# A state-space scan, a 4-bit FFN and a mixture layer in one kernel: contiguous scale and zero-point rows, and output product and expert-input turns moved into the second scan

## What is computed

```
x  = x + ln(mamba(ln(x)))       # conv, selective scan over 512 steps, 1024 x 16 states, gate, y @ W_out.T
x  = x + ln16(gptq_ffn(ln(x)))  # w = q*s[g] - (z[g]+1)*s[g]; down(silu(gate(x)) * up(x)), inner width 1376
x  = x + ln(attention(ln(x)))   # per token, 32 heads of 16
x  = x + ln(moe(ln(x)))
```

## Time and profile before

| | |
|---|---|
| median of 3 runs | 893.2 us (892.1 to 893.83) |
| profiled execution | 893.42 us, its span 891.5 us |
| mean granted TensorE clock | 0.881 |
| TensorE busy | 701.6 us (79%) |
| VectorE busy | 715.8 us (80%) |
| GpSimd busy | 542.7 us (61%) |
| ScalarE busy | 420.6 us (47%) |
| DMA | 86.72 MB, 97 GB/s over the span; 18308 of 65212 packets under 512 B |

### The profile page before, as it was taken

One profiled execution on the slowest core, in us unless ns is written; L12 is line 12 of the kernel. 1 busy time (PEld: TensorE's weight loads), 2 busy tenths in 40 slices (PEclk: granted clock), 3 DMA queues, 4 the chain that ended last, 5 costly groups with the idle time before them and its releaser, 6 DMA issues. The chain is left out here.

```text
span 891.5 us, 8190 instructions
## 1 busy us (share of the span) xinstructions
PE 701.6 (79%) x2700; PEld 316.2 (35%) x2700; DVE 715.8 (80%) x719; ACT 420.6 (47%) x699; POOL 542.7 (61%) x281
## 2 busy tenths in 40 slices
PE   6986669998766978346643499798999978999895
PEld 3322123332211322011110144343445534787774
DVE  4846999989999999999999896988464573676657
ACT  2344776687646764555544224333334343522331
POOL 0008899989989999899999555577002031341152
PEclk9998868999878999567775599899999989999998
DMA  9102423331425432673322067983300020000011
GB/s 277 45 26 102 149 76 100 119 118 56 180 97 183 148 117 84 183 207 118 118 89 77 18 144 193 251 200 79 142 0 1 1 96 0 1 1 1 1 47 48
DMA packets 65212, 86.72 MB, mean 97 GB/s; under 512 B 18308, under 2 KB 32407, under 8 KB 64914
## 3 DMA queue, kind: packets, MB, share of 16 engines
q1 hardware_dynamic: 65170, 86.20, 32.0%
HBM read 74.97 MB, written 11.21 MB: 97 GB/s over the span
## 5 line engine op out<-in xcount | busy, mean ns | idle before, releaser
L1965 POOL TENSOR_TENSOR dbu<-rep_du,bc 128x1024 f32<-128x1024 f32 x128 | 299.0, 2358 | 6.4 <-DVE psum L1066 3.7
L1645 ACT ACTIVATE psum<-rep_dt,aneg 128x512 f32<-128x512 f32 x256 | 166.1, 682 | 148.2 <-DVE hc L1077 118.9
L1066 DVE TENSOR_TENSOR_SCAN psum<-psum,dbu 128x1024 f32<-128x1024 f32 x87 | 198.7, 2284 | 7.7 <-ACT psum L1645 5.1
L845 PE MATMUL psum<-hc,stk 128*32 128x512 f32 x512 | 91.8, 798 | 75.9 <-POOL hc L1974 38.0
L1077 DVE TENSOR_TENSOR hc<-psum,bc 128x1024 f32<-128x1024 f32 x87 | 106.5, 1224 | 3.4 <-PE psum L845 0.4
L1974 POOL TENSOR_TENSOR hc<-hc,bc 128x1024 f32<-128x1024 f32 x41 | 96.5, 2354 | 11.6 <-DVE hc L1066 11.4
L1066 DVE TENSOR_TENSOR_SCAN hc<-psum,dbu 128x1024 f32<-128x1024 f32 x41 | 93.5, 2280 | 6.6 <-ACT psum L1645 4.2
L642 PE MATMUL psum<-xf_hi,gu_hi 128*128 128x512 f16 x176 | 67.7, 385 | 0.0
L642 PE MATMUL psum<-xf_hi,gu_lo 128*128 128x512 f16 x176 | 67.4, 383 | 0.0
L642 PE MATMUL psum<-xf_lo,gu_hi 128*128 128x512 f16 x176 | 67.2, 382 | 0.0
L642 PE MATMUL psum<-xT,w_g 128*128 128x512 f32 x120 | 59.4, 640 | 6.9 <-DVE dt_t L1085 6.9
(11 more groups left out here) (225 smaller groups left out, 1399.1 us busy)
## 6 DMA issues: line engine op xcount, KB each, us to landing
rep_dt<-rep_scratch SPq DMA_DIRECT2D x60, 256.0 KB, 3.3
rep_du<-rep_scratch SPq DMA_DIRECT2D x60, 256.0 KB, 4.3
q_gu<-qgu_in SPq DMA_DIRECT2D x11, 512.0 KB, 4.5
z_gu<-zgu_scratch SPq DMA_DIRECT2D x11, 512.0 KB, 6.6
bc<-bc_scratch SPq DMA_DIRECT2D x16, 256.0 KB, 4.3
rep_scratch<-du_t SPq DMA_DIRECT2D x15, 256.0 KB, 2.0
rep_scratch<-dt_t SPq DMA_DIRECT2D x15, 256.0 KB, 2.3
q_d<-qd_in SPq DMA_DIRECT2D x11, 256.0 KB, 5.0
```

Of the source, the lines that this page charges most:

```text
L845: last = pe.matmul(y_rows(k), stk[:], hc[:, (i + k // 2) % HCS, k % 2, :], start=False, stop=(s == GN - 1))
L1066: dve.tensor_tensor_scan(h, a, dbu[:, i % DBS].rearrange("p e t -> p (e t)"), 0.0, ALU.mult, ALU.add)\
L1645: last = act.activation(psum[:, 2 * (i % 2) + e, :], rep_dt[:, cc % 2, k, :], ACT.Exp, scale=aneg[:, k, c, n:n + 1])
L1965: pool.tensor_tensor(dbu[:, i % DBS], rep_du[:, cc % 2, k:k + 2, :], bc[:, n, :].unsqueeze(1).broadcast_to([P, 2, L]), ALU.mult).then_inc( ...
```

## The change

- Scales and zero points are written once, early, into two scratch arrays with one contiguous row of 1536 values per chunk; a stage has four transfers. There are four slots (`SLOTS`); the fourth lies where batch 1's y was.
- The input of the FFN of batch 0 is normed by ScalarE, turned by TensorE and split by ScalarE and VectorE in scan chunks 13 and 14.
- The output product of batch 1 over inner chunks 0 to 5 (`part`, `PARTS` = 6 of 8) moves into chunks 14 and 15. ScalarE copies it to `obuf`; the other two inner chunks remain at the seam, and VectorE adds the two (`add_partial`).
- The merging of the expert matrices moves one chunk earlier, and its buffers to another place.
- The first `unpack` stands between the last pair and the last `take_y`. Ahead of the first round three chunks are unpacked, not four, and in the rounds VectorE runs `low_weights(i + 2)` and then `unpack(i + 3)`.
- GpSimd does `d_lo` of chunk i-1 after `w_gu` and `w_d` of chunk i. ScalarE waits for `w_gu` and `w_d` separately.
- SyncE loads the attention's weights after the last stage; their two reductions on VectorE stand in round 9, not 7.

The core of the diff:

```diff
+SZ = 2 * KH * P + H
+SLOTS = 4
...
-        (11, 1): [("ft", 0)], (11, 2): [("ft", 1)], (11, 3): [("w1", 0)], (12, 1): [("w1", 1)],
-        (12, 3): [("wr", 0)], (13, 1): [("wr", 1)], (13, 2): [("wr", 2)], (13, 3): [("wr", 3)]}
+        (10, 1): [("ft", 0)], (10, 2): [("ft", 1)], (11, 1): [("w1", 0)], (11, 2): [("w1", 1)],
+        (11, 3): [("wr", 0)], (12, 1): [("wr", 1)], (12, 2): [("wr", 2)], (12, 3): [("wr", 3)],
+        (13, 0): [("tr", "ffn", 0, 0)], (13, 1): [("tr", "ffn", 0, 1)], (13, 3): [("tr", "ffn", 0, 2)],
+        (14, 0): [("tr", "ffn", 0, 3)],
+        (14, 1): [("part", 0)], (14, 2): [("part", 1)], (14, 3): [("part", 2)], (15, 1): [("part", 3)]}
+PARTS = DC - 2
...
+                load(scl[s][:], s_dram[i:i + 1, :].broadcast_to([P, SZ]), ld_stage[s])
+                load(zp[s][:], z_dram[i:i + 1, :].broadcast_to([P, SZ]), ld_stage[s])
...
             for h in range(KH):
                 wait_taken(sp_, ("wr", h))
                 sp_.dma_start(wr_dram[h * P:(h + 1) * P, :], wr_t[h][:]).then_inc(wr_stored, 16)
+            sp_.wait_ge(wr_stored, 16 * KH)
+            stage(1)
...
+            def out_partial(t):
+
+                item = ("part", t)
+                pe.wait_ge(y_taken, DC + PARTS)
+                start(item)
+                product(item, [(u0[:, c, t * P:(t + 1) * P], wout[:, c, :]) for c in range(PARTS)])\
+                    .then_inc(work_ready, 1)
...
+                for t in range(NT):
+                    if i == pair_of(("tr", "ffn", 0, t)) + 3:
+                        low_turned(0, [t])
+            unpack(0)
             take_y(NCH - 1)
...
+            def add_partial(t):
+                item = ("out", 1, t)
+                wait_work(dve, item)
+                wait_taken(dve, ("part", t))
+                dve.tensor_tensor(obuf[1][:, t, :], bank(item), obuf[1][:, t, :], ALU.add)\
+                    .then_inc(taken_sem(item), 1)
+
+            unpack(1)
+            low_weights(0)
             for t in range(NT):
-                norm_tile("ffn", 0, t, xnc)
-            low_turned(0)
-            unpack(0)
-            for i in range(1, 4):
-                unpack(i)
-                low_weights(i - 1)
+                add_partial(t)
+            unpack(2)
+            low_weights(1)
             for i in range(IC):
                 ffn_inner(0, i)
...
-                if i + 4 < IC:
-                    unpack(i + 4)
+                if i + 2 < IC:
+                    low_weights(i + 2)
                 if i + 3 < IC:
-                    low_weights(i + 3)
+                    unpack(i + 3)
...
-                act.wait_ge(w_done, 2 * (i + 1))
-                act.copy(gu_hi[:, i, :], w_gu[i % 3][:]).then_inc(whi_done, 1)
-                act.copy(d_hi[:, i, :], w_d[i % 3][:]).then_inc(whi_done, 1)
+                act.wait_ge(w_done, 2 * i + 1)
+                act.copy(gu_hi[:, i, :], w_gu[i % SLOTS][:]).then_inc(whi_done, 1)
+                act.wait_ge(w_done, 2 * i + 2)
+                act.copy(d_hi[:, i, :], w_d[i % SLOTS][:]).then_inc(whi_done, 1)
...
+            act.wait_ge(exp_done, NPAIR)
+            for i in range(3):
+                high_weights(i)
...
+                pool.wait_ge(q_done, 2 * i + 1)
+                pool.tensor_tensor(w_gu[s][:], w_gu[s][:], z_gu[s], ALU.subtract).then_inc(w_done, 1)
                 pool.wait_ge(q_done, 2 * i + 2)
+                pool.tensor_tensor(w_d[s][:], w_d[s][:], z_d[s], ALU.subtract).then_inc(w_done, 1)
+                if i:
+                    low_down(i - 1)
+            low_down(IC - 1)
```

More of the change, by code:

```diff
@@ L568, in _ @@
             load_rep(DC + 4)
-            wait_taken(sp_, ("gate", 1, DC - 1))
-            stage(1)
             for cc in range(DC + 5, NCH):
@@ L847, in _ @@
                     last.then_inc(nsum_done, 1)
-            for t in range(NT):
-                turn("ffn", 0, t, xnc)
             pe.wait_ge(y_taken, NCH)
@@ L1109, in out_add, with unpack, low_weights, low_turned @@
                 dve.wait_ge(out_done, NB * NT)
+            def unpack(i):
+                s = i % SLOTS
+                dve.wait_ge(ld_stage[s], 64 * (i // SLOTS + 1))
+                dve.tensor_scalar(q_gu[s][:], q_gu[s][:], shift[:, 0:1], 15, ALU.logical_shift_right,
+                                  ALU.bitwise_and)
+                link(dve.tensor_scalar(q_d[s][:], q_d[s][:], shift[:, 0:1], 15, ALU.logical_shift_right,
+                                       ALU.bitwise_and))
+                dve.tensor_tensor(w_gu[s][:], q_gu[s][:], s_gu[s], ALU.mult).then_inc(q_done, 1)
+                dve.tensor_tensor(w_d[s][:], q_d[s][:], s_d[s], ALU.mult).then_inc(q_done, 1)
+            def low_weights(i):
+                dve.wait_ge(whi_done, 2 * i + 1)
+                dve.tensor_tensor(gu_lo[:, i, :], w_gu[i % SLOTS][:], gu_hi[:, i, :], ALU.subtract)\
+                    .then_inc(wlo_gu, 1)
+            def low_turned(b, tiles=range(NT)):
+                for t in tiles:
+                    item = ("tr", "ffn", b, t)
+                    cols = slice(t * P, (t + 1) * P)
+                    dve.wait_ge(xhi_done, NT * b + t + 1)
+                    dve.tensor_tensor(xf_lo[b][:, :, cols], bank(item).rearrange("p (k t) -> p k t", k=KH),
+                                      xf_hi[b][:, :, cols], ALU.subtract).then_inc(taken_sem(item), 1)
+            def low_moe(b):
+                for t in range(NT):
+                    item = ("tr", "moe", b, t)
+                    cols = slice(t * P, (t + 1) * P)
+                    dve.wait_ge(xmhi_done, NT * b + t + 1)
+                    dve.tensor_tensor(xm_lo[b][:, :, cols], bank(item).rearrange("p (k t) -> p k t", k=KH),
+                                      xm_hi[b][:, :, cols].bitcast(F32), ALU.subtract).then_inc(taken_sem(item), 1)
             dve.memset(epst[:, 0:1], EPS).then_inc(eps_ready, 1)
```

171 lines of the change are left out of this document (79 added, 92 removed).

## The result

| | median us | lowest to highest | runs |
|---|---|---|---|
| before | 893.52 | 892.1 to 894.36 | 4 |
| after | 903.35 | 902.95 to 906.96 | 4 |

The changed kernel is **1.21% slower**: the ratio is 1.0121, with a 95% interval of 1.0092 to 1.015. The forecast was 902.6 in 895 to 911. The profiled execution took 902.95 us with a span of 901.1; TensorE's mean granted clock was 0.89.

A forecast was written before the change was run, and what follows sets the result against it. VectorE and GpSimd bound the scan; their turns pace the FFN pass at 8.79 us per chunk. A ring of 10.9 us rounds delays it(10) by 6.7; scan +2.7 makes +9.4: 902.6 us against 893.2, 8-in-10 range 895 to 911.

The forecast's parts named there:

- the term that decides: Weight loop of the first FFN pass: 10.9 us per round against 8.79, it(10) 6.7 us later.
- from the end of an unpack to the end of the next: One round of the first FFN pass, summed through VectorE, GpSimd and ScalarE: 10.9 us against 8.79.
- the ring: First FFN pass: VectorE needs sg(i+1), queued on ScalarE behind d_hi(i+3) of a chunk VectorE just unpacked; 10.9 us per round.
- `it(0)`: VectorE's first `it` of the first FFN pass: at 532.5 us before the scan's shift is added.
- `it(10)`: A late `it` of the first FFN pass: at 642.9 us against 636.32, booked as +6.7, before the scan's shift.
- the scan's shift: The scan's +2.7 us, added last to times given on the clock of before's profiled execution.
- Scan +2.7: Second scan, VectorE: four `xf_lo` at 2.5 us and one tiny operation at 0.2 lengthen the path by 2.7.
- The slower rival: Scan chunks 14 and 15: TensorE's partial products don't fit at low clock; +12 us, 914.6; chance 8%.
- First gate product near 524: TensorE at the seam: starts near 521.7, 20.6 us earlier than before; near 524 with the scan's shift.
- The faster rival: First FFN pass: VectorE's and GpSimd's turns alone set the pace, rounds stay 8.79; 881.5 us; chance 13%.
- In before one transfer was waited for; that wait goes: Contiguous rows and fourth slot: the 3.01 us wait for one transfer goes; nothing more booked.
- I had taken 0 for that at the end of the pass: End of first FFN pass: TensorE at 1.2 GHz after idling would make the last 7.8 us 15; 0 taken, high end +7.

The follow-up runs named there:

- three edits of an order or a wait alone: Changed kernel with sg ahead of gu_hi and d_hi: 893.15 us; with gu_hi waiting for w_d too: 916.5 us; with gu_hi and d_hi behind it_hi: 885.17 us.
- the run with the loop's order alone: Kernel before, with three chunks unpacked ahead instead of four, then gu_lo(i+2) and unpack(i+3) in the loop: 927.54 us, ratio 1.0344.
- the kernel with ScalarE's new order: Changed kernel with gu_hi(i+3) and d_hi(i+3) moved behind it_hi(i+1) in ScalarE's queue, one round later: 885.17 us, ratio 0.9874.
- undoing the order that had visibly changed: Changed kernel with VectorE one chunk further ahead, as in the kernel before (unpack(i+4) and gu_lo(i+3) in the loop): 898.04 us, ratio 1.0012.

## Why the prediction was right

**The mechanism and the term that decides** held. The step "from the end of an unpack to the end of the next", 10.9 us, measured 10.79. Its parts, predicted and measured: `w_gu` 2.25 and 2.21, `w_d` 1.26 and 1.23, `d_hi` 0.59 and 0.65, `sg` 0.65 and 0.53, `it` to `it_lo` 1.42 and 1.43, `it_lo` 0.61 and 0.61, `gu_lo` 1.14 and 1.14, unpack 3.0 and 2.99. That the ring is the cause, and not only beside it, is shown by three edits of an order or a wait alone: they shorten it (9.45, where its sum gave 9.5), lengthen it (11.73 for 11.9), or open it (8.79).

**`it(0)` and `it(10)`.** With the scan's shift `it(0)` was to start at 535.2 and started at 535.27; `it(10)` was to come at 645.6 and came at 645.78, 9.46 late for 9.4 (642.9 less 636.32 is 6.6, not the 6.7 in the sum, so 9.3 by its own terms). In between, the ends of unpack(4), (5), (6) and (10) were forecast at 561.3, 575.1, 587.3 and 630.9 with that shift, and are 561.4, 575.1, 587.3 and 630.5 (each the end of the unpack's `w_d`). The last `gu_lo`, forecast near 638, starts at 637.17. The stretch behind the last `it_lo` was 8.6 us for TensorE's 7.8.

**Scan +2.7**: measured 2.77, but that it is so close is luck. The four `xf_lo` cost 2.39, for 2.5. The one tiny operation, put at 0.2, cost 0.98. VectorE in the changed kernel, where the next instruction starts at 409.15:
```profile
408.17 1.06 DVE L1268 SCALAR_TENSOR_TENSOR fnmr<-mv,rstd 128x4 f32<-128x4 f32 x1
```

That makes 3.4. The changed kernel's profile was 0.6 us ahead at the same scan instruction just before (404.70 against 405.31), and the sum is 2.77. Such a lead is drift between executions: the run with the loop's order alone has the code of before up to the seam, and takes y 2.8 us before it (506.23 against 509.04). No stall was added: from 100 to 512 us VectorE's waits sum to 7.3 us, and to 7.9 in the kernel before without the 2.06 ahead of y. The slower rival, parts that don't fit, did not come: the four parts' records took 5.42 to 6.48 us, under the 7 from which it was to decide.

**First gate product near 524**: 524.47.

**The faster rival**, that the turns of VectorE and GpSimd alone set the pace, was the right description of the kernel with ScalarE's new order: rounds of 8.79, 885.17 us where the rival had 881.5. It fell for the reason given against it, that `sg(i+1)` stands behind `d_hi(i+3)`. By the rule of the Trainium skill on engines that exclude each other (SBUF — State Buffer, Who interferes with whom) the round could not rise; it rose, because the ring is made of order and not of exclusion. Where the ring is open, the rule describes the rest well, `it` at 0.68 and `it_lo` at 1.42.

**Wrong in detail.** "`w_gu` at 2.3 to 2.4" was 2.73: it starts 0.5 us earlier, under the unpack's last operation, and ends where I had it. "In before one transfer was waited for; that wait goes" credits the contiguous rows: alone they leave it at 3.00 us. It went with the loop's order. That nothing was booked for either saved the sum. And I did not see that TensorE would wait for `sg` too:
```profile
PE psum L645 <- ACT sg L1860: 25.3, 8, 6.1
```

Its next product needs the bank that `sg` reads, so it waits 25.3 us in eight places, which split the work between gate and up. After such a wait of 2.90 us at 602.80 the granted clock over the next 4.2 us is 0.61 and products take 0.63 us in place of 0.38, the level of 1.2 GHz; I had taken 0 for that at the end of the pass. At the end it was 0: the gap beside `it(8)`, ahead of the products at 635.15, was 1.24 us, and they took 0.38 to 0.39. Inside the pass the slow stretches cost nothing: the round behind the slow products at 602.80 took 10.79 us (602.78 to 613.57), and the next, whose products started after a wait of 1.16 and took 0.38, took 10.78.

## What to carry to other kernels

When a step is moved on one engine, write down the whole closed path from that step to its own next turn, through every queue that it passes, and sum it: the engines' busy shares say nothing of it (VectorE was busy 92% before and 54% after). In each in-order queue ask what stands behind an instruction that now waits for something fresh; the repair can be two instructions in a third engine's queue, here worth 20 us on the span, where undoing the order that had visibly changed gave half of it. Judge a bundle by its parts: on the span from y to `it(10)` the loop's order alone loses 32.4 us, and the split wait gives back 8.5, the moved product 14.0, the moved turns 5.7 and the rows nothing. That leaves 4.2 of the measured 5.9, though each part was taken out of a different kernel and need not add up; GpSimd's new order, the fourth slot and the attention's loads weren't run alone. All of it stood behind one ratio of 1.0121.
